# Adding C-weighted pair products into y: a GpSimd tensor addition, or an accumulating transfer issued from GpSimd

## What is computed

```python
def step(carry, inp):
    a, bu, c = inp
    carry = a * carry + bu
    y = jnp.einsum('bdn,bn->bd', carry, c)
    return (carry, y)
...
return y + u * D[:, None]
```

## Time and profile before

| | us |
|---|---|
| time, median of 3 runs | 3374.95 (3372.26 to 3375.04) |
| span of the profiled execution, first to last instruction | 3372.2 |
| DVE busy | 2905.3 |
| PE busy | 2679.9 |
| ACT busy | 2349.2 |
| GpSimd busy | 1850.2 |

### The profile page before, as it was taken

One profiled execution on the slowest core, in us unless ns is written; L12 is line 12 of the kernel. 1 busy time (PEld: TensorE's weight loads), 2 busy tenths in 40 slices (PEclk: granted clock), 3 DMA queues, 4 the chain that ended last, 5 costly groups with the idle time before them and its releaser, 6 DMA issues.

```text
span 3372.2 us, 43844 instructions
## 1 busy us (share of the span) xinstructions
PE 2679.9 (79%) x12290; PEld 1952.8 (58%) x12290; DVE 2905.3 (86%) x3648; ACT 2349.2 (70%) x3653; POOL 1850.2 (55%) x1028
## 2 busy tenths in 40 slices
PE   4456887878888788887878888787888878888898
PEld 1224565665656556575655656565565656656676
DVE  3998989989898998989899898998989899898940
ACT  3875785768678576876867777586777857686732
POOL 0435575565656556565565656456565655656742
PEclk7567998898988888998889898898899989899899
DMA  1841222222222222222222222222222222222323
GB/s 55 295 151 45 90 86 89 87 87 86 86 95 91 79 88 92 91 86 88 90 87 80 93 95 78 95 86 94 79 86 94 86 87 89 87 87 85 113 96 107
DMA packets 156483, 317.17 MB, mean 94 GB/s; under 512 B 17824, under 2 KB 18208, under 8 KB 156080
## 3 DMA queue, kind: packets, MB, share of 16 engines
q1 hardware_dynamic: 119344, 246.86, 22.0%
q10 hardware_dynamic: 36864, 67.13, 6.5%
HBM read 281.93 MB, written 31.98 MB: 93 GB/s over the span
## 4 chain that ended last, share of the span: by engine, by line
DVE 43%; PE 24%; issue 19%; ACT 10%; POOL 1%; DVEq 1%; ACTq 1%; DMA 0%; SPq 0%; POOLq 0%
DVE scan_ps L774 20%; PE ffn_ps L475 13%; DVE hC L785 4%; PE scan_ps L365 3%; DVE y L798 3%; DVE delta L835 3%; ACT dB L611 2%; DVE gate L891 2%; PE misc_ps L456 2%; PE misc_ps L404 2%; ACT dA L602 2%; PE misc_ps L419 2%; DVE delta L829 1%; PE misc_ps L370 1%; DVE x L865 1%
## 5 line engine op out<-in xcount | busy, mean ns | idle before, releaser
L957 POOL TENSOR_TENSOR y<-y,hC 128x1024 f32<-128x1024 f32 x512 | 1236.2, 2415 | 1305.2 <-DVE hC L785 1304.0
L774 DVE TENSOR_TENSOR_SCAN scan_ps<-dA,scan_ps 128x512 f32<-128x512 f32 x1024 | 1248.2, 1219 | 26.1 <-ACT dA L602 14.8
L365 PE MATMUL scan_ps<-ident,dB 128*128 128x128 f32 x4096 | 716.9, 307 | 437.7 <-DVE hC L785 428.4
L365 PEld LDWEIGHTS scan_ps<-ident,dB 128*128 128x128 f32 x4096 | 533.6, 156 | 713.8 <-DVE hC L785 553.0
L611 ACT ACTIVATE dB<-duT,bT 128x512 f32<-128x512 f32 x1024 | 725.7, 711 | 138.3 <-PE scan_ps L365 137.6
L785 DVE TENSOR_TENSOR hC<-scan_ps,c_rows_sb 128x512 f32<-128x512 f32 x1024 | 708.4, 692 | 73.2 <-DVE scan_ps L774 1.0
L602 ACT ACTIVATE dA<-delta,a_neg 128x512 f32<-128x512 f32 x1024 | 709.8, 711 | 58.5 <-DVE hC L785 57.5
L475 PE MATMUL ffn_ps<-hb_hi,ring 128*128 128x512 f32 x1536 | 686.7, 447 | 21.1 <-POOL hb_lo L979 15.5
L475 PE MATMUL ffn_ps<-hb_lo,ring 128*128 128x512 f32 x1536 | 639.5, 416 | 0.0
L475 PE MATMUL ffn_ps<-ha_hi,ring 128*128 128x512 f32 x1024 | 439.3, 429 | 2.4 <-POOL ha_lo L979 2.4
L475 PE MATMUL ffn_ps<-ha_lo,ring 128*128 128x512 f32 x1024 | 406.3, 397 | 0.0
(11 more groups left out here) (89 smaller groups left out, 3166.5 us busy)
## 6 DMA issues: line engine op xcount, KB each, us to landing
ring<-split_weights SPq DMA_DIRECT2D x704, 256.0 KB, 2.7
c_rows_sb<-c_rows ACTq DMA_DIRECT2D x256, 256.0 KB, 3.3
xt<-x_tok SPq DMA_DIRECT2D x32, 512.0 KB, 4.2
x<-ffn_w SPq DMA_DIRECT2D x22, 512.0 KB, 5.7
split_weights<-ha_hi SPq DMA_DIRECT2D x22, 512.0 KB, 2.7
split_weights<-ha_lo SPq DMA_DIRECT2D x22, 512.0 KB, 4.0
out_tok<-out_st SPq DMA_DIRECT2D x16, 512.0 KB, 2.9
inw<-in_wT SPq DMA_DIRECT2D x1, 1024.0 KB, 4.7
```

Source lines behind the costliest of these rows:

```text
L365: mm = nc.tensor.transpose(dst[:, j * P:(j + 1) * P], src(j), ident[:])
L774: nc.vector.tensor_tensor_scan(scan_ps[:, s % 4], dA[:, s % DA_RING], scan_ps[:, s % 4], 0.0, ALU.mult, ALU.add).then_inc(scan_done, 1)
L957: nc.gpsimd.tensor_tensor(y2[:, par, c:c + 2, :], y2[:, par, c:c + 2, :], hC[:, p % 2], ALU.add).then_inc(y_added, 1)
```

## The change

GpSimd no longer reads `y2` and `hC` and writes `y2` itself. It issues a transfer that reads `hC[:, p % 2]`, adds it to the two channel tiles of `y2` and writes them, 512 KB for each pair. The transfer tells its end by adding 16 to a semaphore; since two may be in flight, each of the two `hC` buffers has its own, `y_added[0]` and `y_added[1]`. `y_add_begun` is counted and nothing waits for it. The three waits stay where they were and wait for the landing of the transfer instead of the end of the instruction.

```diff
-        hC_done, y_added = sem("hC_done"), sem("y_added")
+        hC_done = sem("hC_done")
+        y_added = [sem(f"y_added{i}") for i in range(2)]
+        y_add_begun = sem("y_add_begun")
...
                 if s % 2 == 0:
-                    wait_past(dve, y_added, r * PAIRS + (p - 1))
+                    wait_past(dve, y_added[p % 2], r * (8 * PAIRS) + 16 * (p // 2))
...
                 if p >= 2:
-                    pool.wait_ge(y_added, r * PAIRS + (p - 1))
+                    pool.wait_ge(y_added[p % 2], r * (8 * PAIRS) + 16 * (p // 2))
                 c = 2 * (p % 2)
-                nc.gpsimd.tensor_tensor(y2[:, par, c:c + 2, :], y2[:, par, c:c + 2, :], hC[:, p % 2], ALU.add
-                                        ).then_inc(y_added, 1)
+                pool.sem_inc(y_add_begun, 1)
+                pool.dma_start(y2[:, par, c:c + 2, :], hC[:, p % 2], accum_op=ALU.add).then_inc(y_added[p % 2], 16)
 
             def gate_tile(r, par, c):
                 if c == 0:
-                    pool.wait_ge(y_added, r * PAIRS + PAIRS)
+                    for k in range(2):
+                        pool.wait_ge(y_added[k], r * (8 * PAIRS) + 8 * PAIRS)
```

## The result

| | before | changed |
|---|---|---|
| median of 4 runs, us | 3374.99 (3372.26 to 3375.21) | 3272.88 (3268.47 to 3277.41) |
| span of the profiled execution, us | 3372.2 | 3267.8 |

The changed kernel is faster by 102 us: the ratio is 0.9701, interval 0.9688 to 0.9715. The direction is the predicted one and the time lies in the range, but the gain is twice the predicted 50 us, so a term of the sum is off.

A forecast was written before the change was run, and what follows sets the result against it. DVE, busy 86%, was taken to bound the kernel, held by GpSimd's additions. Terms A, B, C, D: -100 - 15 + 45 + 20 = -50 us against the 3372.2 span, so 3325 us; range 3265 to 3368, 8 in 10 3240 to 3510.

The forecast's parts named there:

- term A: GpSimd's additions no longer hold DVE's SBUF work (L865, L821, L823, L835): -100 us, bounds -70 and -124.
- Term B: Step 11: shorter GpSimd queue ahead of the last gate tile, for which PE's output projection waits: -15 us, bounds 0 and -18.
- Term D: Making the transfer's descriptors on GpSimd may hold DVE like an addition: +20 us, bounds 0 and +60.
- L: Time from GpSimd's start of the transfer to its landing: 6.0 us, low bound 3.1, high bound 11.4.
- term C: DVE's first C product of pair p+2 waits for pair p's landing in dense places: +45 us, bounds 0 and some +220.
- Rival 1: The adding is cheap, landing within 5 us, and the issue doesn't hold DVE: 3233 to 3260 us; chance 0.20.
- Rival 5: Gain and stalls cancel to within some microseconds; chance 0.06.
- Rival 2: DVE's wait for the landing takes over; slower, 3503 us at a landing time of 8 us; chance 0.28.
- Rival 3: The issue costs GpSimd as much as the addition did, 2.4 us or more: 3483 us; chance 0.10.
- Rival 4: The transfers' traffic delays PE's weights: no more than 20 us, no case of its own and no chance given.

The follow-up runs named there:

- the run without the five pairs: Kernel before, with pairs 9, 22, 24, 26 and 27 of each row adding only the first column: 3223.12 us, ratio 0.9547.
- the plain copy: Changed kernel with the transfer lacking `accum_op`, so y is overwritten, not added to: 3212.62 us, ratio 0.9523.

## Why the prediction was right or wrong

**Read rightly: the mechanism.** The chain gives GpSimd 1%, and still its additions cost 180 us, most of it through DVE. The two durations of one shape, from which term A was made, were the right evidence, and the long forms vanished as said.

**The failed step: the size of term A (-100 us, bounds -70 and -124).** The measured share of the five additions is -152 us (148 by the scan tiles of the traces), outside the bounds. The prediction had 25 us at step 19, 40 at steps 54 and 55 and 35 at steps 44 to 50; the run without the five pairs shows 25.5, 55.7 and 48.2, and 16.2 more at steps 0 to 3. Three assumptions failed.
First, "DVE's delay also holds PE there, so I take 35, between 28 and 58.6". DVE's operations lost 48.2 us in steps 44 to 51, and all 48.2 became time. I had read PE's 18.27 of 20.00 us as a floor for a stretch that I had cut too narrow; over steps 44 to 51 PE has 22.74 of 28.38 us and 5.6 to spare.
Second, "I count nothing" for the low parts, and the assumption that their share of the excess is small and stays. I looked for excess only where an addition lies over a DVE operation. Pair 26's addition alone costs 21 us through the low parts behind it: 15.3 us in L835 into gate (32 x 477 ns), 15.0 in L840 (64 x 234 ns), and PE's 13.4 us of waiting. That is why steps 52 to 55 gave 55.7 where I had 40.3. The other way round, half of L823's excess (15.5 of 31.2 us) stays without the additions; in the changed kernel it is gone too, and no run shows why the low parts miss L823 there.
Third, steps 0 to 3 stood at nothing. Their 16.2 us fit DVE's wait for ACT's gate, which went from 137.2 to 122.6 us; I had not looked at it, and no run takes it apart, so this part stays open.
The excess of the four groups that I counted came out near in the changed kernel, 112 us of 124, with L835 into out_st at 28.9 where I had 40.3. But I had not compared L835 into gate (15.3), L840 (14.7), L804 (10.4), L846 (6.0) and L767 (5.0) at all, 51 us more.

**Term B (-15)** was right: the gate tile's place alone is worth 18 us, and PE's wait fell to 3.5 us, under the 5 foretold.

**Term D (+20) was nothing.** L867 and L823 run beside an issue in 412 and 417 ns, and those L867 that start inside one in 426. The issue takes 0.87 us, not 1.3.

**L and term C (+45).** L was 5.6 from the issue against 6.0 (the prediction's other estimates, 3.2 and 4.4 us, were too low: the plain copy already takes 4.2). Pairs 7, 21 and 27 wait 20.6, 19.7 and 23.4 us in all, 1.2 to 1.5 each, where L - 4.9 gave 1.1. But pairs 1, 5, 31, 25 and 3 wait as well, 21.3, 20.5, 16.3, 12.0 and 9.5 us, and with the smaller ones there are 193 us where I had 53. They cost far less, since many replace other waits (137.2 to 59.0 us for ACT's gate): the transfer's whole price is 78 us against 65 in C and D. So the sum of C and D came near by luck, from other parts: no hold, 26 us in the first row (I had 10 for the first pairs of a row and the last row together), 38 in rows 1 to 14, 12 at the end.

**The rivals.** Rival 1 (3233 to 3260) did not come true, though its doubt about the hold did; L above 4.9 was real. Rival 5 (no change) is out at 102 us. Rivals 2 and 3 fail at their conditions, L of 6.7 and an issue of 2.4 us. Rival 4 is not seen as PE's wait for its weights; the traffic shows in the landings of the weights' loads instead, and most of all in the first row. The adding transfers themselves take as long when there are few: 5.5 us in the run with five pairs by transfer.

**The ledger:** -180 (predicted -115) + 78 (predicted +65) = -102 (predicted -50).

**What stays open:** why the time won at steps 0 to 3 came with the five pairs; of the 29 us between the adding and the plain transfer in rows 1 to 14, how much is the later landing and how much the fuller DMA engines; no run here changes one alone. A third `hC` buffer was not tried.

## What to carry to other kernels

- An engine with 1% of the chain can still set the time: compare the mean duration of one operation on one shape between its places, and look in the order of time at what the neighbour engine does while it is long.
- Before work moves to another resource, try to move it in time: 5 of 32 additions made 152 of 180 us, and holding those back gained 163 us with the gate tile, more than the transfers' 102.
- Price a colliding instruction by its queue as well: what it pushes onto others, and who waits for that. And price a new wait by what already waits there: with 129 us of landing waits gone, DVE's idle time fell by 49.
- Before one engine's load is taken as a floor for another's gain, measure the whole stretch between two points that both pass: PE had 18.27 of 20.00 us in the cut that the prediction chose, and 22.74 of 28.38 over steps 44 to 51, where all that DVE lost in length became time.

## What the runs showed of the hardware

- A transfer that adds from SBUF to SBUF keeps the DMA engines twice as long as the same plain copy (44.5% against 21.6% of the span for the same 73728 packets), with a landing of 5.6 against 4.2 us; the issue takes 0.87 against 0.56 us. A packet of about 4 KB takes 328 ns (median) where it adds and 159 where it copies. The median landing hardly depends on how many there are: with 80 adding transfers in place of 512, their queue at 7.2% of the span, it is 5.5 us.
- GpSimd's own SBUF operations slow down beside adding transfers. The low parts (mean ns):

```profile
L982 POOL TENSOR_TENSOR ha_lo<-x,ha_hi 128x512 fp32r<-128x512 f32 x256 | 361.6, 1514 | 77.9 <-ACT ha_hi L694 50.2 <-ACT ha_hi L707 13.9 <-issue 13.4
```

They take 1514 ns against 1283 before, and 1286 beside plain copies. Within the trace of the changed kernel, the 24 of them during which no adding packet was in flight and no issue ran take 1298 ns on the mean, and the 109 beside adding packets but no issue 1512. What in the transfer slows them wasn't isolated.
- GpSimd instructions that follow one another closely, an issue among them, can hold one DVE operation through all of them (0.42 us became 3.45, in the run with a transfer for each tile).
